# Wide-head attention of a decoder: TensorE's step in a new order, V copied in two halves

## What is computed

```python
q, k, v = split_heads(x @ Wq), split_heads(x @ Wk), split_heads(x @ Wv)
q, k = apply_rope(q), apply_rope(k)
sim = jnp.einsum('bid,bjd->bij', q, k) * scale
sim = jnp.where(causal[None], sim, -jnp.inf)
attn = jax.nn.softmax(sim, axis=-1)
out = jnp.einsum('bij,bjd->bid', attn, v)
x = x + out @ Wo + bo
```

## Time and profile before, and how to read it

| what | value |
| --- | --- |
| runs | 1885.44, 1889.69, 1890.20 us; median 1889.69 |
| the profiled execution's own span | 1940.8 us |
| granted TensorE clock, mean of the span | 0.929 of full speed |
| busy share of the span | PE 85%, DVE 76%, POOL 72%, ACT 50% |
| wide-head stage | from 780 to about 1525 us of the span |
| DMA queue of SP's transfers (q1) | 140528 packets, 24.9% of 16 engines |

### The profile page before, as it was taken

How to read it: one execution, slowest core, us unless ns; L and a number is a source line. 1 busy time by engine, 2 the same in 40 slices (tenths; PEclk the granted TensorE clock), 3 DMA queues, 4 the chain that set the end, 5 groups by cost and what they waited for, 6 DMA issues and landing times. The chain is left out here.

```text
span 1940.8 us, 63428 instructions
## 1 busy us (share of the span) xinstructions
PE 1657.9 (85%) x24717; PEld 1377.0 (71%) x24719; DVE 1471.5 (76%) x3151; ACT 961.1 (50%) x2012; POOL 1406.9 (72%) x1253
## 2 busy tenths in 40 slices
PE   4999999999998826699999999999998689267776
PEld 2777777777776725577777888888887579267675
DVE  6888888888886771688998888888887566845454
ACT  3677777777774322354445444444444441234343
POOL 3777777877785455688989988888887358656655
PEclk9999999999997957799999999999999789678888
DMA  8000032000000042444443443343343156521211
GB/s 248 10 7 8 8 120 73 18 17 15 15 16 3 1 136 70 104 120 114 120 120 96 97 97 97 97 97 96 96 98 83 52 180 197 161 69 58 61 55 41
DMA packets 155071, 154.03 MB, mean 79 GB/s; under 512 B 37246, under 2 KB 106944, under 8 KB 154160
## 3 DMA queue, kind: packets, MB, share of 16 engines
q1 hardware_dynamic: 140528, 130.91, 24.9%
q0 software_dynamic: 6704, 15.61, 2.8%
q10 hardware_dynamic: 7696, 5.71, 1.1%
HBM read 58.77 MB, written 26.71 MB: 44 GB/s over the span
## 5 line engine op out<-in xcount | busy, mean ns | idle before, releaser
L1437 POOL TENSOR_TENSOR wa_rot<-wa_rot,wa_cross 128x1024 f32<-128x1024 f32 x128 | 305.3, 2385 | 51.1 <-DVE wa_cross L1649 50.8
L412 POOL TENSOR_TENSOR sa_sd<-sa_sd,sa_mx 128x1024 f32<-128x1024 f32 x128 | 243.5, 1903 | 133.1 <-DVE sa_mx L648 132.2
L592 ACT ACTIVATE sa_sd<-sa_sd 128x1024 f32<-128x1024 f32 x128 | 135.7, 1060 | 114.5 <-POOL sa_sd L412 111.5
L1646 DVE TENSOR_TENSOR wa_rot<-wa_ps_qk,cos 128x1024 f32<-128x1024 f32 x128 | 155.7, 1217 | 40.2 <-PE wa_ps_qk L1503 40.1
L1602 ACT COPY wa_pt<-wa_ps_svt 128x1024 f32<-128x1024 f32 x64 | 64.9, 1014 | 229.4 <-PE wa_ps_svt L1539 229.4
L648 DVE TENSOR_REDUCE sa_mx<-sa_sd 128x16 f32<-128x1024 f32 x128 | 156.2, 1220 | 4.4
L1443 POOL TENSOR_TENSOR wa_sd<-wa_sd,wa_mx 128x1024 f32<-128x1024 f32 x64 | 121.9, 1905 | 38.2 <-DVE wa_mx L1662 38.2
L534 PEld LDWEIGHTS sa_ps_o<-sa_vbd,sa_pt 128*64 128x64 f32 x4096 | 132.9, 140 | 19.7 <-issue 12.0
L534 PE MATMUL sa_ps_o<-sa_vbd,sa_pt 128*64 128x18 f32 x4096 | 145.7, 214 | 0.8 <-DVE sa_o L675 0.8
L1503 PE MATMUL wa_ps_qk<-wa_xt,l_wk 128*128 128x128 f32 x1024 | 133.5, 284 | 11.7 <-DVE wa_cross L1649 11.6
L419 POOL TENSOR_TENSOR sa_km<-sa_k,head_mask 128x512 f32<-128x512 f32 x128 | 135.4, 1058 | 7.3 <-ACT sa_k L583 6.9
(11 more groups left out here) (312 smaller groups left out, 4311.9 us busy)
## 6 DMA issues: line engine op xcount, KB each, us to landing
wa_whole<-wa_rot SPq DMA_DIRECT2D x1024, 64.0 KB, 2.0
choice_dram<-sa_zero_rows SPq DMA_DIRECT2D x32, 256.0 KB, 3.4
choice<-choice_dram SPq DMA_DIRECT2D x32, 256.0 KB, 3.6
x_res<-in_x_dram SPq DMA_DIRECT2D x16, 256.0 KB, 6.8
sa_ctx_t<-in_ctx_t_dram SPq DMA_DIRECT2D x64, 64.0 KB, 1.8
c_index<-in_index_dram SPq DMA_DIRECT2D x2, 2048.0 KB, 7.8
xn_dram<-c_xn SPq DMA_DIRECT2D x16, 256.0 KB, 2.9
cs_ctx_t<-in_ctx_t_dram SPq DMA_DIRECT2D x16, 256.0 KB, 3.0
```

What stands on the lines that cost most here:

```text
L412: pool.tensor_tensor(sd[:, v % 4], sd[:, v % 4], mx[:, v % 4].unsqueeze(2).to_broadcast([P, H0, SEQ]), ALU.subtract).then_inc(sub_ready, 1)
L592: act.activation(sd[:, v % 4], sd[:, v % 4], ACT.Exp, scale=scale).then_inc(p_ready, 1)
L1437: pool.tensor_tensor(rot[n][:, v % 2], rot[n][:, v % 2], cross[n][:], ALU.add)\
L1646: dve.tensor_tensor(rot[n][:, v % 2].rearrange("p f j t -> p (f j) t"), src.rearrange("p f j t -> p (f j) t"), bc(k.cos[:], 1, 2 * QUADS), ...
```

## The change

PE's step becomes queries, out_project, x transpose, P transpose, keys, V, values, scores. Scores of a tile run one step earlier, at the end of the step; V one step later. V's semaphore now counts halves, and ACT copies each half of V by itself, with the exponential between the two. `project_v` waits for the mask of the same tile, `scores` for the V copy of the tile before. The diff's parts are, in turn, POOL's step, PE's stages and step, ACT's stages and step, and DVE's step. POOL's order becomes subtract_max, both rotations, divide, add_bias, own_product; DVE masks first and takes the maximum after rotate(0).

```diff
-                for stage, behind in ((rotate(1), 2), (divide, 4), (add_bias, 5), (rotate(0), 1), (subtract_max, 3),
-                                      (own_product, 6)):
+                for stage, behind in ((subtract_max, 3), (rotate(0), 1), (rotate(1), 1), (divide, 3), (add_bias, 4),
+                                      (own_product, 5)):
...
             def project_v(i, t, v):
-                if late(t, 1):
-                    pe.wait_ge(s_taken, t)
+                pe.wait_ge(s_taken, t + 1)
                 for b in range(2):
                     for half in range(2):
                         mm = pe.matmul(ps_svt[half * SEQ:(half + 1) * SEQ, b], xt[:, v, b * SEQ:(b + 1) * SEQ],
                                        k.l1_wv[:, half], start=True, stop=True)
-                mm.then_inc(v_made, 1)
+                    mm.then_inc(v_made, 1)
 
             def scores(i, t, v):
                 pe.wait_ge(moved[0][v % 2], 16 * PIECES + 8 * PIECES * (t - v % 2))
-                pe.wait_ge(v_ready, t + 1)
+                if late(t, 1):
+                    pe.wait_ge(v_ready, t)
...
-                for stage, behind in ((project(0), 1), (out_project, 5), (x_transpose, 0), (scores, 3), (project(1), 1),
-                                      (p_transpose, 4), (project_v, 2), (values, 4)):
+                for stage, behind in ((project(0), 1), (out_project, 5), (x_transpose, 0), (p_transpose, 4),
+                                      (project(1), 1), (project_v, 3), (values, 4), (scores, 2)):
...
-                    act.wait_ge(v_made, t - 3)
+                    act.wait_ge(v_made, 2 * (t - 3))
...
-            def v_copy(t, v):
-                act.wait_ge(v_made, t + 1)
+            def first_v_copy(t, v):
+                act.wait_ge(v_made, 2 * t + 1)
                 if late(t, 2):
                     act.wait_ge(ot_made, t - 1)
-                act.copy(v_sb[:, v % 2], v_ps).then_inc(v_ready, 1)
+                act.copy(v_sb[:, v % 2, 0], v_ps[:, 0])
+
+            def second_v_copy(t, v):
+                act.wait_ge(v_made, 2 * t + 2)
+                act.copy(v_sb[:, v % 2, 1], v_ps[:, 1]).then_inc(v_ready, 1)
...
-                for stage, behind in ((o_copy, 5), (v_copy, 3), (normalise, 0), (x_copy, 0), (p_copy, 4), (exponential, 3)):
+                for stage, behind in ((o_copy, 5), (normalise, 0), (x_copy, 0), (p_copy, 4), (first_v_copy, 3),
+                                      (exponential, 3), (second_v_copy, 3)):
...
+                when(mask, 3)
                 when(rotate(0), 1)
...
+                when(maximum, 3)
                 when(residual, 5)
-                when(mask, 3)
-                when(maximum, 3)
```

## The result

| | before | changed |
| --- | --- | --- |
| median, us | 1889.95 | 2001.3 (four runs, 1993.83 to 2007.65) |
| ratio, 95% interval | 1 | 1.0581 [1.0545, 1.0618] |
| the profiled execution: its time, its span | span 1940.8 | 1993.83, span 1992.0 |
| wide-head stage in the profiled execution | 741.7 | 847.8 |

The kernel became 5.8% slower: 111 us. Slower was forecast, but 2001 lies above the range of 1908 to 1970. The two spans differ by 51, the forecast's +55; the two medians by 111. So the first question is where the profiled execution of the kernel before had spent 51 us that its other runs had not, and the second why the stage is 106 us longer and not 55.

What follows compares the result with a forecast made beforehand. The prediction took PE to bound the kernel, at 10.78 us a steady step. Its terms, 26 + 25 + 6 - 2 = +55 us on the median of 1889.69, gave 1945 us, with 1908 to 1970 for 8 in 10.

Steps and rivals of the forecast that it cites:

- PE's own work: PE's step in the wide-head stage: fewer tile-shape changes save 0.18 us, so PE alone would need 10.60 a step.
- What the new order waits for: Chain from queries through rotation add and 16 SP DMA issues to scores: 23.0 us over two steps, 11.5 a step.
- rival of the second V copy: ACT's second V copy, behind the exponential, releases scores: steps of 11.1 us with the loop edge, total 1914; chance 0.16.
- I put the difference on the median: Base of the total: +55 us added to the runs' median 1889.69, not to the profiled span 1940.8, giving 1945.
- The first rival: Long chain shorter without the profiler, so ACT's split V copy binds: +24 us, total 1914; chance 0.16.
- The first 23 steps: Tiles 4 to 27: pair_up and scalings delay the rotation add, 25.25 us per pair of steps; +25 us.
- The last 36 steps: Tiles 27 to 63: steps of 11.55 us instead of 10.83, from the two-step transfer chain; +26 us.
- Fill and drain: Stage's start and end: pair_ups ahead of the first rotation add, +6 us; last tile's scores come sooner, -2 us.
- Worse: First 23 steps: loads in SP's queue delay late moves too, another +15 to +25 us, total 1965; chance 0.06.

Runs made afterwards that it cites:

- copies_then_exp: Changed kernel with both V copies ahead of the exponential on ACT; 2042.69 us, ratio to before 1.0463.
- add_before_max: Changed kernel with POOL's first rotation add ahead of subtract_max again; 1962.14 us, ratio to before 1.0369.
- max_first: Changed kernel with DVE's maximum ahead of rotate(0); 1973.17 us, ratio to before 1.0432.
- pair_late: Changed kernel with POOL's pair_up, in even steps of the first part, behind both rotations instead of ahead of subtract_max; 1965.09 us, ratio to before 1.0361.
- keep_busy: Changed kernel with four more useless matmuls a step on PE between values and scores; 2026.77 us, ratio to before 1.0442.
- before_again: Kernel before, unchanged, profiled in one more execution; 1899.81 us.
- before_act_loads: Kernel before with the group loads of later steps issued by ACT instead of SP; 1914.57 us, ratio to before 1.0126.
- short_loop: Changed kernel with maximum ahead of rotate(0), exponential ahead of first V copy, pair_up behind both rotations, PE's loop kept; 1980.91 us, ratio to before 1.0202.
- flat_pe: Changed kernel with PE's first 60 steps written out instead of 8; 2052.67 us, ratio to before 1.0613.
- exp_first: Changed kernel with DVE's maximum ahead of rotate(0) and ACT's exponential ahead of the first V copy; 2005.38 us, ratio to before 1.0314.
- before_flat: Kernel before with PE's first 60 steps written out instead of 8; 1982.52 us, ratio to before 1.0228.

## Why the prediction was wrong in size and right in kind

- **PE's own work**, 0.18 a step less: right in its parts. In the changed kernel x transpose to P transposes is 0.11 and P transposes to keys 0.87, as worked out. The shortest steps of copies_then_exp (from the queries of tiles 21 and 25) take 10.55, against 10.60 worked out; in its steady stretch the short step is 10.72, where keys and V come 0.09 later each. None of it reached the total.
- **What the new order waits for**, 23.0 for two steps: right, 22.95, its terms within 0.02 us but for the issues (0.3 too long) and the start of scores behind the landing (0.15 too short), which nearly cancel. add_before_max, max_first and copies_then_exp each change one link and move what they should. The rival of the second V copy was right for one step in two (11.05 forecast, 11.06 seen): the chains alternate, which neither case had said. The average is the two-step loop's.
- **"I put the difference on the median"**: right as a method, but my step before it, "no row tells where those lie", left the 51 us in the same doubt as the terms. The first rival took them for the profiler's and drew the range down to 1908. They lay in a stage that the change doesn't touch, at clock 0.85, and a second profile of the same kernel would have shown it. So the stage's +106 and the medians' +111 agree. That the two spans differ by 51, near the forecast's 55, is chance: the slow last stage of the one hides half of the stage's loss in the other.
- **The first 23 steps, +25**: the step that failed; it measured +61.7. The pairs of steps from tile 16 to 22 take 25.9, 26.3 and 25.4 against 25.25; the others are longer, such as tiles 4 to 9, which take 14.3 a step. I had priced every block at its length at the full clock, while the chain itself makes waits of 2 to 3 us here; behind most of those, PE runs at half clock and passes the delay on to the next pair. Two of the stalls fall in this part as well (steps of 19.9 and 19.6 us). pair_late gets 26 us of it back, keep_busy 23.
- **The last 36 steps, +26**: mis-sized; it measured +36.8. Tiles 27 to 42 take 11.49 a step and 48 to 63 take 11.56 (forecast 11.55). The five steps of 42 to 47, behind one stall, take 70.1 instead of 57.7. That one episode is 12.4 us, more than the whole difference.
- **Fill and drain, +6 and -2**: +7.9 and -0.3.
- **"Worse", the queue of SP, +15 to +25**: it named the loads, and they were not it. From tile 5 to 23 the transfers release the scores of odd tiles, and SP starts those issues within 0.03 us of the end of the rotation add, with no load in between. SP's issues were lengthened beside instruction fetches, 28.7 us in all against 11.3 before. Only part of that is on the path: for the odd tiles 5 to 17, first to last issue takes 9.8 to 10.8 instead of 9.4, some 7 us together.

The excess over the forecast is 51 us in the stage. Excess at the low clock (33 - 8 = 25), the stalls (5.90 + 4.77 + 5.10 = 16) and long issues (28.7 - 11.3 = 17) add to 58, and they overlap, since behind each stall the clock is down and long issues stand beside its fetches. So the three are of the size of the excess, but neither that they make up all of it nor a share for each is shown. What triggers a stall at the loop's edge stays open: none in three profiles of the order before with its loop (before, before_again, before_act_loads), two to four in each profile of the new one with its loop, but none in keep_busy's, where PE has no idle time in the steady state. PE's idle time by itself doesn't decide it: before_act_loads stands idle for 1.5 us a step from tile 4 to 20 and keep_busy for 1.2, without a stall, while short_loop stalls three times in steady steps with 0.3 us of idle time. What stands last in the loop (scores in place of values) and how long the loop's code is changed too, and no run takes these apart.

The Trainium skill (DMA: Bandwidth & Descriptors, Issuing engines are not separate DMA queues) has an issuing engine's time to initiate a DMA as usually small beside the DMA itself. The trace agrees for a single one, 0.59 against a landing of 2.0. But 16 of them in a row are the longest link of the chain, 9.4 us in front of that 2.0.

## What to carry to other kernels

An order that makes PE's own work shorter can still lengthen the step: before moving a consumer earlier, sum the chain from its producer over as many steps as it spans, and compare with what PE leaves it; here 18.8 us of chain had 6.6 to spare and the new place took them all. Then price the wait that results, since a wait on PE behind which its clock is down costs the work behind it as well, and in a chain over two steps it returns. And before a difference is put on a base, compare the base's profiled span with the times of its other runs, and where they differ, find the stage; a second profile of the unchanged kernel tells.

## What the runs showed of the hardware

- Behind a wait of 2.58 us ahead of scores, scores took 1.98 and queries 3.78 instead of 1.16 and 2.05; behind most waits of 1.9 they kept their length. The kernel before did the same behind its one wait of 2.82. It isn't a sharp bound: in flat_pe scores took 1.98 behind 2.09, and 1.16 behind 3.00 with the next queries at 2.05 too. Over all profiles there are 18 waits of over 3.1 us ahead of scores; behind 16 the scores were lengthened, and behind the other two (exp_first 3.16, short_loop 3.80) the block after them, out_project, with 3.68.
- Beside an instruction fetch one of SP's DMA issues takes mostly 1.0 to 1.9 us instead of 0.59 (0.87 us more on average over the 95 long ones of before_flat). Writing a loop out, 80 more fetches in the stage, made the kernel before 2.3% slower (1.0228 [1.0198, 1.0258]) without an instruction changed.
- PE can stand 5 us at the edge of a loop with no semaphore to wait for; two instruction fetches start inside the stall and seven follow, at other tiles in each execution.
- The same last stage took about 195 or 239 to 246 us, at clock 0.96 or 0.85 in the two windows shown; all profiles of one sitting agree, and nothing here tells why.
